# GpSimd's expert part: loop written out, marking operation removed, record transfers two per step, last landings awaited by SyncE

## The reference

```python
x = x + tanh(g_xattn[0]) * xattn(layernorm(x), ctx, ctx)     # 16 heads of 64, 64 keys per batch
x = x + tanh(g_ffn[0])   * ffn(layernorm(x))                 # mixture of experts

# ffn: 8 experts, each 256 -> 1024 -> 256, the best 2 per token
logits = xt @ gate_w.T
w_topk, sel = top_k(logits, 2);  w_topk = softmax(w_topk)
h = silu(einsum('td,edf->tef', xt, w1));  y = einsum('tef,efd->ted', h, w2)
out = einsum('td over its two experts, weighted by w_topk')
```

## Time and profile before

| | us |
|---|---|
| median of 3 runs | 782.55 (781.37 to 789.14) |
| span of the profiled execution | 779.1 |
| median less this span | 3.45 |
| PE busy | 740.5 (95%) |
| DVE busy | 609.3 (78%) |
| ACT busy | 381.4 (49%) |
| POOL busy | 422.0 (54%) |
| the 71 scatter-adds (L1681), busy | 148.5 (mean 2.09) |

### The profile page before, as it was taken

The page is one execution under the profiler, slowest core; times in us unless marked ns, Lnnn a source line. Parts: engine busy times, 40 slices in busy tenths (PEclk is TensorE's granted clock), DMA queues, the critical chain, the costliest instruction groups (busy, mean ns, idle before and its releaser), DMA issues. The chain is left out here.

```text
span 779.1 us, 23891 instructions
## 1 busy us (share of the span) xinstructions
PE 740.5 (95%) x8058; PEld 618.1 (79%) x8059; DVE 609.3 (78%) x1310; ACT 381.4 (49%) x675; POOL 422.0 (54%) x379
## 2 busy tenths in 40 slices
PE   7999999999999999988999998999999999999991
PEld 6577777777777677756898987899999999999991
DVE  5788889898999989796777778677767777777750
ACT  3686766766676766644435342233333333333330
POOL 5145445667576767554434848445555555555542
PEclk9999999999999999999999999999999999999996
DMA  7451534535262817233878874433333333333321
GB/s 295 148 175 71 183 116 150 196 116 193 111 226 75 272 48 242 85 109 117 237 205 218 238 189 91 66 51 50 48 50 50 49 50 48 51 51 50 50 29 21
DMA packets 93178, 93.89 MB, mean 121 GB/s; under 512 B 59312, under 2 KB 77936, under 8 KB 92720
## 3 DMA queue, kind: packets, MB, share of 16 engines
q1 hardware_dynamic: 31184, 64.97, 24.9%
q0 software_dynamic: 13392, 18.03, 13.4%
q10 hardware_dynamic: 48528, 9.92, 7.1%
HBM read 53.89 MB, written 37.95 MB: 118 GB/s over the span
## 5 line engine op out<-in xcount | busy, mean ns | idle before, releaser
L1427 PE MATMUL h_ps<-bx_h,w_now 128*128 128x128 f16 x2272 | 194.0, 219 | 6.5 <-DVE bx_l L1564 6.2
L1440 PE MATMUL pair_ps<-weights,ht_h 128*128 x1136 | 190.6, 273 | 2.0 <-DVE ht_l L1578 1.9
L1427 PEld LDWEIGHTS h_ps<-bx_h,w_now 128*128 128x128 f16 x2272 | 152.2, 98 | 10.9 <-DVE bx_l L1564 8.8
L1681 POOL DMA_INDIRECT out<-y,meta x71 | 148.5, 2092 | 16.0 <-issue 8.5
L1427 PE MATMUL h_ps<-bx_l,w_now 128*128 128x128 f16 x1136 | 156.3, 219 | 0.0
L1440 PE MATMUL pair_ps<-weights,ht_l 128*128 x568 | 154.9, 273 | 0.0
L1680 POOL TENSOR_TENSOR wait_mark<-wait_mark 128x1 f32<-128x1 f32 x71 | 37.6, 529 | 159.0 <-DMA out<-y,meta 102.1
L1440 PEld LDWEIGHTS pair_ps<-weights,ht_h 128*128 128x128 f16 x1136 | 109.9, 97 | 17.3 <-issue 2.7
L1251 POOL TENSOR_TENSOR r_l<-r,r_h 128x512 f16<-128x512 f32 x62 | 72.3, 1166 | 94.8 <-ACT r_h L828 93.5
L1505 ACT ACTIVATE y<-pair_ps,meta 128x256 f32<-128x256 f32 x71 | 33.7, 474 | 171.4 <-DVE meta L1559 75.2
L1576 DVE CAST ht_h<-hid 128x1024 f16<-128x1024 f32 x71 | 49.5, 697 | 73.3 <-ACT hid L1498 73.3
(11 more groups left out here) (274 smaller groups left out, 1336.9 us busy)
## 6 DMA issues: line engine op xcount, KB each, us to landing
stage<-in_w SPq DMA_DIRECT2D x16, 1024.0 KB, 8.7
w_split<-split SPq DMA_DIRECT2D x14, 1024.0 KB, 5.9
weights<-w_split SPq DMA_DIRECT2D x14, 1024.0 KB
rows<-records ACTq DMA_DIRECT2D x268, 32.0 KB
xin<-in_x SPq DMA_DIRECT2D x7, 512.0 KB, 5.4
x_even<-in_x SPq DMA_DIRECT2D x4, 512.0 KB, 3.6
x_odd<-in_x SPq DMA_DIRECT2D x4, 512.0 KB, 3.5
out<-x_even SPq DMA_DIRECT2D x4, 512.0 KB, 2.7
```

The source lines that it names most:

```text
L1427: last = nc.tensor.matmul(h_ps[r % 2][:, c, :], w1_now[:, r % 2, s, k * F + c * P:k * F + c * P + P], xt[:, r % 2, k, :], start=(j == 0 an ...
L1440: last = nc.tensor.matmul(y_ps[r % 2], ht[:, r % 2, c, :], weights_at(e, s, WN // 2 + c * D, D).rearrange("p o n -> p (o n)"), start=(c == ...
L1681: pool.indirect_dma_start(out, bass.IndirectOffsetOnAxis(meta[:, r, 0:1].bitcast(U32), 0), y[:, r % 2, :], None, compute_op=ALU.add).then_ ...
```

## The change

GpSimd no longer uses `run`. All 71 steps are written out in its own loop of Python, so that every wait is on a constant. The marking operation, its buffer's clearing and its semaphore are removed, and the two waits (on y and on the landing before) stand directly ahead of the scatter-add. Each group's eight record transfers are issued two per step in jobs 7, 8, 9 and 10. The reciprocal root of group 6 follows block 0's scatter-add instead of preceding it. The waits for the last landings are on SyncE, at the end of its stream, no longer on GpSimd. The other engines' programs stay as they are.

```diff
-    wait_mark = carry.wait_mark
...
-    mark_set = sem("mark_set")
...
     @block.sync
...
         sp.wait_ge(x1_stored, 16)
         sp.wait_ge(pads_in, 16 * E)
+        sp.wait_ge(carried_in, 16 * LEFT)
+        sp.wait_ge(records_in, 2 * 2 * TG * 16)
+        sp.wait_ge(added, 16 * NB)
...
     @block.gpsimd
         def step(i, r):
             pool.wait_ge(y_out, i + 1)
             after(pool, added, i * 16)
-            pool.wait_ge(mark_set, i + 1)
-
-            nc.gpsimd.tensor_tensor(wait_mark[:, 1:2], wait_mark[:, 0:1], wait_mark[:, 0:1], ALU.add).then_inc(mark_set, 1)
             pool.indirect_dma_start(out, bass.IndirectOffsetOnAxis(meta[:, r, 0:1].bitcast(U32), 0), y[:, r % 2, :], None,
                                     compute_op=ALU.add).then_inc(added, 16)
...
         def routing(j, i):
+            if j == 0 and i == -1:
+                ln2_rstd_of(0)
             if j == 1 and i == -2:
                 ln2_rstd_of(1)
-            if i in (7, 8, 9):
+            if i in (7, 8, 9, 10):
                 if i == 7:
                     pool.wait_ge(routed.slots_done, j + 1)
                     pool.wait_ge(rec_done, j + 1)
-                for n in range(3 * (i - 7), min(3 * (i - 6), 2 * TG)):
+                for n in range(2 * (i - 7), 2 * (i - 6)):
                     scatter(rec[j], slot[j], n, records_in)
...
-        nc.gpsimd.memset(wait_mark[:, :], 0.0).then_inc(mark_set, 1)
         for n in range(2 * TG - LEFT, 2 * TG):
             scatter(carry.rec, carry.slot, n, carried_in)
-        ln2_rstd_of(0)
-        run(pool, step, routing, everything_there)
-        pool.wait_ge(carried_in, 16 * LEFT)
-        pool.wait_ge(records_in, 2 * 2 * TG * 16)
-        pool.wait_ge(added, 16 * NB)
+        for i in range(NB):
+            step(i, i % RB)
+            if i < HEAD:
+                for j in range(2):
+                    routing(j, i - 1 - j * BEHIND)
+            if i == HEAD - 1:
+                everything_there()
```

## The result

The changed kernel takes 773.74 us (median of 6 runs, 772.31 to 778.40), the kernel before on the same chip 782.87 us (781.37 to 789.14, 6 runs). The ratio on record is 0.9897, 95% interval 0.9858 to 0.9937; it is an estimate of its own and not the quotient of the two medians, which is 0.9883. On the scale of the prediction it makes 774.5 us (0.9897 x 782.55), a gain of 8.1 us (4.9 to 11.1 by the interval) where 4.8 were forecast. 774.5 is also the lower end of the range that the prediction gave. A second measurement on another chip gave 775.34 us against 784.07, ratio 0.9914 (0.9883 to 0.9945).

What follows compares the result with a forecast made beforehand. TensorE was taken as full in the regular stretch, GpSimd's lag on the path only at the end. Gains 4.3 + 0.5 = 4.8 us off a 779.1 span, plus 3.45, made 777.7 us; range 774.5 to 782.0.

Steps and rivals of the forecast that it cites:

- The tail: At the kernel's end, with GpSimd's lag gone, the last scatter-add starts at 764.5 or 764.6 instead of 768.91: gain 4.3 us.
- d: Dispatch time of a scatter-add that waits itself, ahead of its start: taken as 0.3 us, bounds 0 and 0.64.
- The last y right behind the last matmul: Sign of being right, at the kernel's end: y's idle time near 1 us, not 3.80.
- rival A: GpSimd's lag survives the mark's removal, scatter-adds held from ht_l to behind w_now in a repeating cycle: 781.2 us, chance 0.21.
- The end: Last waits moved to SyncE, 6.60 us behind the last landing left as they are: 0, bounds -1 to +1.
- rival C: Behind the last landing, GpSimd's own finish comes off the end: some 2 to 3 us more, 775 us, chance 0.10.
- much less than 6.6 us behind the last landing: Sign of being wrong, at the program's end: GpSimd's own finish would have come off the 6.60 us.
- The records: Ahead of the loop, two record transfers per step let the matmuls start earlier: gain 0.5 us, bounds 1.36 and -1.5.
- The root: Reciprocal root queued behind block 0's scatter-add: cost 0, with 2 us of cover before its reader on VectorE.
- B: In the regular stretch GpSimd becomes the pace setter through y's two buffers: slower, about 809 us, chance 0.05.

Runs made afterwards that it cites:

- the kernels of the 24 blocks: The changed kernel with 24 instead of 20 written-out blocks: late table spread over six jobs, ratios 0.9887 and 0.9883; table unspread, 776.18 us, ratio 0.9928.

## Why the prediction was right, and where it wasn't

**The tail: right in size and place.** 4.3 us forecast, 4.2 measured, with d at 0.27 to 0.28 behind y. Where a scatter-add waits for a landing instead, it starts 2.89 us behind its predecessor's end, against 2.26 + 0.3 = 2.56 in the sum. The last one starts 1.84 us behind the last matmul, forecast 1.8. (The bounds given for d = 0.64 and d = 0 were 4.0 and 5.0; by the same sum they are 3.9 and 5.1.) "The last y right behind the last matmul" held (0.04 us); its idle time is 2.91 us and not near 1, since that counts from the end of the y before, at 758.02. I had mixed the two up; nothing hung on it.

**The tail: wrong in its reason.** The step says that with the mark gone the chain needs 4.1 us per block, catches up 1.2 us per block and then stays. The mark put back left it free too (0.9911), and so did the whole old loop in one execution. Even in the free pattern the lag shrinks by 0.6 us per block and not by 1.2 (2.70 us at block 21, 0.31 at block 25), since the next scatter-add starts 2.9 to 3.0 us behind the end of one and not 2.56, and two of these four are still held (1.93 us against 1.55). What the runs showed is the condition I gave under rival A and weighed only there: two patterns, each of which keeps itself up, and one moment that picks. I had it as "the lag must be 3 us or more when the records are through", and that was about right; measured, the line is the start of ht_l, 2.9 to 3.4 us behind y at block 21. In the regular stretch no catching up takes place behind that line, as the kernels of the 24 blocks show with no mark in them. So rival A's mechanism exists in the changed kernel as well, and it escaped by half a microsecond in each of two profiles. That the tail's 4.3 us came in full in the profiled execution is in part luck. Nor is it shown that the change makes the free pattern the usual one: it is free in 7 of 9 profiles of its kind, against 1 of 5 of the old kind, but 8 free ones among 14 would by chance alone leave one or none to five given profiles in about 6 of 100 cases, and the profiles are of different kernels.

The rows also say what became of the hold-up. In the changed kernel the scatter-add at 573.02 ends 1.43 us behind w_now's end (573.73), the one at 578.43 1.42 us behind it (578.98): both are held, but once, for 0.42 to 0.59 us over 1.55, and the mean of 1.90 against 1.55 makes 0.35 us a block, where GpSimd waits for y anyway. The Trainium skill ("SBUF — State Buffer", section "SBUF: two separate sides") says that VectorE and GpSimd hold the port they share for a whole instruction; the hold-up did move to w_now by that rule, as rival A had it. The trace agrees: each of the 38 scatter-adds that start inside w_now between 510 and 735 us ends 1.42 to 1.45 us behind w_now's end, however long before it started. What neither the rule nor I had is that it shrinks from two holds per block to one once the phase is right. Taken as "it moves and doesn't go", the rule gave 1.3 us.

**The end: the term that was mis-sized.** "Waits on SyncE at the end: 0, bounds -1 to +1", with rival C at 0.10 for 2 to 3 us. Measured 2.4 us, outside those bounds and inside rival C's, in 14 of 14 profiles on the side of the engine that waits; "much less than 6.6 us behind the last landing" was named as a sign of being wrong, and it came. I saw no instruction in those 6.60 us and took that as neither for nor against. It should have weighed more: the change swaps the engine that finishes last. What GpSimd does in that time no row shows.

**The records: right in mechanism, the whole head too small.** bx_h is gated by the last record's landing, 490.62 against the 491.5 to 492.0 forecast, and the gap there falls by 0.57 us (forecast 0.5). But the gap falls only with the mark gone: with marks and two records per step it is 2.19 and 2.21 us. Two pairs of runs say 3 to 4 us for the records' edit alone, and its own trace doesn't show them. The traces of the whole change show 2.5 to 3.6 us between block 2 and block 23, of which the gap is 0.3 to 0.6; how the rest divides between mark and records is open. So is whether two per step makes the free pattern more frequent, worth 4.2 us each time. The parts can't all be added up either: 2.4, 4.2 and 3 to 4 us make 9.6 to 10.6, and the change is worth 8.1 (4.9 to 11.1).

**The root:** 0, with 2.2 us of cover, as forecast. **B** (GpSimd sets the pace): TensorE is busy for all 225.00 us of the stretch.

The sum of 4.8 us was 3.3 short by the ratio and 3.8 by the spans. 2.4 of that is the end; the other 0.9 to 1.4 lies ahead of the loop. The range held 774.5 only as its last value, and only because it was stretched to rival C "with a little more at the head": that is what came.

A version that spreads the late table takes 3.5 us of TensorE's gaps away (3.8 to 0.3) and gave 0.9887 and 0.9883 to the changed kernel's 0.9897 and 0.9914. The four intervals overlap, so that it beats the changed kernel is suggested, not shown.

## What to carry to other kernels

When an engine off the critical path lags by a constant, ask which phase it is locked to and what put it there, not which of its instructions is slow: taking an instruction out may do little but move the moment that picks the pattern, and one profile shows only one of them. Look at what awaits the last landing: moving that wait to another engine was worth 2.4 us for three lines. And where two executions of one kernel differ by 3 us in a stretch, do not price an edit in that stretch from one pair of traces; cut the stretch first, and see in which part of it they differ.

## What the runs showed of the hardware

- The time behind the last DMA traffic depends on the engine that awaits it: 4.3 to 4.5 us with SyncE, 6.7 to 6.9 us with GpSimd, 14 profiles.
- An indirect DMA on GpSimd starts 0.27 to 0.28 us after the end of ScalarE's instruction that releases it, where nothing else keeps it waiting.
- A scatter-add that starts inside ht_l ends 0.07 to 0.13 us behind the w_now that follows (2.55 us long in the row above), in all 152 cases from 510 to 735 us in the five held profiles with w_now in one piece; one that starts 0.47 and 0.64 us into w_now ends 1.43 and 1.42 us behind it. With w_now in two halves some end in the seam instead (2.51 us long, 0.52 us ahead of the pair's end).
- TensorE has gaps of 0.2 to 1.2 us between matmuls that nothing in the trace releases, between 373 and 490 us (DMA is busiest from 371 to 455). From block 0's first matmul to block 2's it took 8.7 to 8.9 us in the five profiles that have none of these gaps there, 10.4 to 13.9 us in the nine that have them. What they are wasn't tried.
